# A decoder layer on one core: the scaling of the output weights, the copy of the inverse and two convolution taps take other places in their queues

## What is computed

```python
mixed = silu(causal_conv4(x @ w_qkv))        # 8192 channels: q, k (16 heads), v (32 heads)
z = x @ w_z                                  # 32 heads of 128
beta = sigmoid(x @ w_b)
g = -exp(A_log) * softplus(x @ w_a + dt_bias)
q, k = l2norm(q) * 128 ** -0.5, l2norm(k)    # each serves two heads of v
for t in range(128):                         # per sequence and head, S is 128 x 128
    S = S * exp(g[t])
    delta = (v[t] - k[t] @ S) * beta[t]
    S = S + outer(k[t], delta)
    o[t] = q[t] @ S
og = o * silu(z)
on = og * rsqrt(mean(og * og) + 1e-6) * norm_w
return on @ w_out                            # 4096 -> 256
```

## Time and profile before

| | before |
|---|---|
| median of 3 runs | 2258.57 us (2254.74 to 2260.40) |
| profiled execution, its own time | 2255.11 us |
| its span, first to last instruction | 2253.2 us |
| granted TensorE clock, mean | 0.970 |
| busy: PE, PEld | 93%, 76% |
| busy: DVE, ACT, POOL | 76%, 67%, 40% |
| ticks n=8 to 71 | 158 us to about 1722 us of the span |

### The profile page before, as it was taken

The page is one execution under the profiler, slowest core; times in us unless marked ns, Lnnn a source line. Parts: engine busy times, 40 slices in busy tenths (PEclk is TensorE's granted clock), DMA queues, the critical chain, the costliest instruction groups (busy, mean ns, idle before and its releaser), DMA issues.

```text
span 2253.2 us, 49295 instructions
## 1 busy us (share of the span) xinstructions
PE 2091.6 (93%) x18636; PEld 1716.1 (76%) x18636; DVE 1711.3 (76%) x2944; ACT 1512.7 (67%) x3585; POOL 904.1 (40%) x714
## 2 busy tenths in 40 slices
PE   4659999999999999999999999999988899999998
PEld 4448888888888888888888888887776476666776
DVE  6789797887879788787977978787325777767665
ACT  4547777777777777777777677775767666565632
POOL 1534454444445445445535534532333123213232
PEclk8779999999999999999999999998999999999999
DMA  3432322322232332233233222212243012322232
GB/s 77 94 73 48 89 44 72 63 64 67 55 85 46 72 75 49 68 60 80 52 70 72 48 70 56 75 34 56 58 137 133 1 66 76 104 94 73 91 136 85
DMA packets 274633, 161.56 MB, mean 72 GB/s; under 512 B 209352, under 2 KB 246752, under 8 KB 269280
## 3 DMA queue, kind: packets, MB, share of 16 engines
q1 hardware_dynamic: 274400, 158.41, 27.6%
HBM read 122.43 MB, written 35.91 MB: 70 GB/s over the span
## 4 chain that ended last, share of the span: by engine, by line
issue 36%; POOL 26%; PE 23%; DVE 8%; ACT 4%; DMA 2%; SPq 2%; POOLq 0%; DVEq 0%; ACTq 0%
POOL SM L577 5%; POOL EB L493 5%; POOL Q L555 5%; PE ps L1739 4%; POOL SZ L579 3%; PE ps L1347 3%; POOL EB L497 3%; PE ps L1349 3%; PE ps L1348 3%; POOL WL L471 2%; POOL SM L585 2%; PE ps L1660 1%; ACT SC L856 1%; PE ps L1651 1%; PE ps L1480 1%
## 5 line engine op out<-in xcount | busy, mean ns | idle before, releaser
L909 DVE SCALAR_TENSOR_TENSOR A<-ps,CW,A 128x508 f32<-128x508 f32 (+2 forms) x768 | 515.9, 734 | 55.3 <-ACT A L671 50.1
L572 POOL TENSOR_SCALAR SM<-SM 128x8 f32<-128x8 f32 x64 | 12.6, 196 | 813.8 <-ACT DL L690 813.8
L1480 PE MATMUL ps<-WO,DL 128*128 128x256 f32 x1008 | 244.5, 394 | 39.5 <-POOL WO L484 24.5
L1480 PEld LDWEIGHTS ps<-WO,DL 128*128 128x128 f32 x1008 | 189.7, 194 | 74.5 <-POOL WO L484 26.4
L1347 PE MATMUL ps<-XH,WH 128*128 128x512 f32 x512 | 221.5, 433 | 26.7 <-DVE A L909 25.8
L1127 DVE TENSOR_TENSOR SZ<-SZ,ps 128x512 f32<-128x512 f32 x128 | 87.7, 687 | 201.5 <-PE ps L1514 201.4
L1349 PE MATMUL ps<-XH,WL 128*128 128x512 f32 x512 | 206.4, 403 | 0.0
L1348 PE MATMUL ps<-XL,WH 128*128 128x512 f32 x512 | 205.2, 401 | 0.0
L690 ACT ACTIVATE DL<-SZ 128x128 f32<-128x128 f32 x512 | 152.4, 298 | 38.5 <-PE ps L1514 28.8
L856 ACT ACTIVATE SC<-ps,A 128x128 f32<-128x128 f32 x512 | 141.7, 386 | 51.5 <-DVE A L1252 50.7
L1112 DVE TENSOR_TENSOR BP<-ps,EB 128x512 f32<-128x512 f32 x256 | 158.3, 681 | 3.3 <-ACT EB L665 3.3
(11 more groups left out here) (225 smaller groups left out, 5556.1 us busy)
## 6 DMA issues: line engine op xcount, KB each, us to landing
EB<-decay_rows SPq DMA_DIRECT2D x128, 256.0 KB, 4.7
WE<-expert_halves SPq DMA_DIRECT2D x32, 1024.0 KB, 5.1
x_blocks<-BP SPq DMA_DIRECT2D x256, 32.0 KB, 1.7
X<-x_blocks SPq DMA_DIRECT2D x16, 512.0 KB, 6.5
tt_blocks<-TI SPq DMA_DIRECT2D x16, 512.0 KB, 2.6
tn_blocks<-TM SPq DMA_DIRECT2D x16, 512.0 KB, 2.6
TTF<-tt_blocks SPq DMA_DIRECT2D x256, 32.0 KB, 1.9
expert_halves<-BP SPq DMA_DIRECT2D x8, 1024.0 KB, 5.8
```

What stands on the lines that cost most here:

```text
L909: dve.scalar_tensor_tensor(acc, ps(i, 0, [[128, 4], [1, 128 - s]]), at(CW, tile * 4 + 3 - s, [[1, 1]]), acc, ALU.mult, ALU.add).then_inc(s ...
L1480: t = pe.matmul(ps(7 - i, b * 256, [[1, 256]]), at(on_buf(k), (4 * i + 2 * b + v) * 128, [[1, 128]]), at(WO, v * 256, [[1, 256]]), start=( ...
```

## The change

It moves the output weights WO by one tick. Their load is issued in ticks with k%4==3 (the last step that uses the old ones), at the end of SP's list for that tick, where it waits for that step's projections; before, it came first in the next tick. Their scaling on POOL is in the same tick, behind the decays and ahead of the norm section of step m. The power sk (L585) also goes ahead of the norm section. On ScalarE the copy of the inverse into TM goes from between the two on_T copies to behind the TTF copy. On DVE the taps kq_tap(n+1, 1) go from behind the gates to ahead of them, and kq_tap(n+1, 2) from the start of the next tick to the same place; the pumps' rooms are 5260 and 800 in place of 4060 and 2000 in the ticks below 64, and for n of 64 and more the same as before.

```diff
@@ -392,8 +392,6 @@
                 for n in range(NT):
                     m, k = n - LAG3, n - LAG4
                     vn = m + 1
-                    if 0 < k < NSTEP and k % 4 == 0:
-                        load_wo(k // 4)
                     if n % 4 == 0 and 4 <= n <= NSTEP:
                         load_x(n // 4 - 1)
                     if 0 <= m < NSTEP and m % 4 == 1 and m // 4 + 1 < HK:
@@ -411,6 +409,8 @@
                         store_x(n)
                     if n + 3 < NSTEP:
                         load_rows(n + 3)
+                    if 0 <= k and k % 4 == 3 and k + 1 < NSTEP:
+                        load_wo(k // 4 + 1)
                     if n == NSTEP + 1:
                         load_raw(0)
                         load_raw(1)
@@ -553,14 +553,21 @@
                         if n:
                             pool.wait_ge(sem["nq_mm"], n)
                         pool.tensor_tensor(at(Q2, 0, full), at(buf, 0, full), at(buf, 0, full), ALU.mult).then_inc(sem["sq"], 1)
-                    if 0 < k < NSTEP and k % 4 == 0:
-                        scale_wo(k // 4)
                     if EARLY - 1 <= n and n + 2 < NSTEP:
                         decay(n + 2)
                     if n == 5:
                         split_lo("v", W_V, 0)
                         split_lo("z", W_Z, 0)
                         scale_wo(0)
+                    if n % 4 == 0 and 4 <= n <= NSTEP:
+                        j = n // 4 - 1
+                        pool.wait_ge(sem["nk"], j + 1)
+                        if j >= 2:
+                            pool.wait_ge(sem["vv"], 4 * (4 * j - 4))
+                        pool.tensor_tensor(at(SM, C_SK + (j % 2) * 16, [[4, 4], [1, 4]]), at(SM, C_NK, [[4, 4], [1, 4]]),
+                                           at(SM, C_PH, [[0, 4], [1, 4]]), ALU.pow).then_inc(sem["sk"], 1)
+                    if 0 <= k and k % 4 == 3 and k + 1 < NSTEP:
+                        scale_wo(k // 4 + 1)
                     if m == NSTEP - 1:
                         pool.wait_ge(sem["ld_ctx"], 16)
                         pool.tensor_copy(at(EB, 0, [[9, 128], [1, 8]]), at(TI, 0, [[8, 128], [1, 8]])).then_inc(sem["cc"], 1)
@@ -577,13 +584,6 @@
                         pool.tensor_tensor(rr, xs, at(SM, C_MH, [[1, 8]]), ALU.pow).then_inc(sem["rr"], 1)
                         pool.wait_ge(sem["rr"], m + 1)
                         pool.tensor_tensor(szp, szp, at(SM, C_RR, [[1, 8], [0, 128]]), ALU.mult).then_inc(sem["on"], 1)
-                    if n % 4 == 0 and 4 <= n <= NSTEP:
-                        j = n // 4 - 1
-                        pool.wait_ge(sem["nk"], j + 1)
-                        if j >= 2:
-                            pool.wait_ge(sem["vv"], 4 * (4 * j - 4))
-                        pool.tensor_tensor(at(SM, C_SK + (j % 2) * 16, [[4, 4], [1, 4]]), at(SM, C_NK, [[4, 4], [1, 4]]),
-                                           at(SM, C_PH, [[0, 4], [1, 4]]), ALU.pow).then_inc(sem["sk"], 1)
                     if NSTEP - 4 <= k < NSTEP - 2:
                         x1_pow(k % 4)
                     if m == NSTEP - 2:
@@ -801,15 +801,15 @@
                         decay_exp(n + 1)
                     if s4 and k < NSTEP - 1:
                         on_T(k, 0)
+                    if s4 and k < NSTEP - 1:
+                        on_T(k, 1)
+                    if s3:
+                        act.wait_ge(sem["tt128"], m + 1)
+                        act.activation(at(TTF, 64, [[128, 8], [1, 64]], 0, 64), ps(6, 0, [[64, 8], [1, 64]], 0, 64),
+                                       ACT.Copy).then_inc(sem["tt128_sb"], 1)
                     if sv and vn % 4 == 0:
                         act.wait_ge(sem["inv"], INV_OPS * (vn // 4 + 1))
                         act.activation(at(TM, 0, [[1, 32], [32, 32]]), at(TI, 0, [[32, 32], [1, 32]]), ACT.Copy).then_inc(sem["tn"], 1)
-                    if s4 and k < NSTEP - 1:
-                        on_T(k, 1)
-                    if s3:
-                        act.wait_ge(sem["tt128"], m + 1)
-                        act.activation(at(TTF, 64, [[128, 8], [1, 64]], 0, 64), ps(6, 0, [[64, 8], [1, 64]], 0, 64),
-                                       ACT.Copy).then_inc(sem["tt128_sb"], 1)
                     if EARLY <= n and n % 2 and n + 1 < NSTEP:
                         decay_exp(n + 1)
                         decay_exp(n + 2)
@@ -1157,7 +1157,7 @@
                     vn = m + 1
                     s1, s3, s4, sv = n < NSTEP, 0 <= m < NSTEP, 0 <= k < NSTEP, 0 <= vn < NSTEP
                     rate = 1 if s1 else 2
-                    if s1 and (n > EARLY or n == 0):
+                    if s1 and n == 0:
                         kq_tap(n, 2)
                     if s1:
                         if n > EARLY or n == 0:
@@ -1168,8 +1168,10 @@
                         norm_rows(n - 1)
                     if n % 4 == 0 and 4 <= n <= NSTEP:
                         norm_sums(n // 4 - 1)
-                    pump(2500)
-                    pump(1560)
+                    if s1:
+                        pump(5260)
+                    else:
+                        pump(4060)
                     if sv:
                         v_tap(vn, 1)
                     if n % 4 == 0 and 4 <= n <= NSTEP:
@@ -1194,7 +1196,13 @@
                         y_add(k, 0)
                     if s4 and k < NSTEP - 2:
                         y_add(k, 1)
-                    pump(2000)
+                    if s1:
+                        pump(800)
+                    else:
+                        pump(2000)
+                    if EARLY <= n and n + 1 < NSTEP:
+                        kq_tap(n + 1, 1)
+                        kq_tap(n + 1, 2)
                     if s3:
                         gate(m, 0)
                     if s3:
@@ -1204,8 +1212,6 @@
                             apply_x1(0)
                     if NSTEP - 4 <= k < NSTEP - 2:
                         norm_x1(k % 4)
-                    if EARLY <= n and n + 1 < NSTEP:
-                        kq_tap(n + 1, 1)
                     if m == NSTEP - 2:
                         dve.wait_ge(sem["bias_tr"], 1)
                         dve.tensor_copy(q(0, [[1, 32]]), ps(3, 0, [[1, 32]])).then_inc(sem["bias_T"], 1)
```

More of the change, by code:

```diff
@@ L803, in _ @@
                         on_T(k, 0)
-                    if sv and vn % 4 == 0:
-                        act.wait_ge(sem["inv"], INV_OPS * (vn // 4 + 1))
-                        act.activation(at(TM, 0, [[1, 32], [32, 32]]), at(TI, 0, [[32, 32], [1, 32]]), ACT.Copy).then_inc(sem["tn"], 1)
                     if s4 and k < NSTEP - 1:
@@ L812, in _ @@
                                        ACT.Copy).then_inc(sem["tt128_sb"], 1)
+                    if sv and vn % 4 == 0:
+                        act.wait_ge(sem["inv"], INV_OPS * (vn // 4 + 1))
+                        act.activation(at(TM, 0, [[1, 32], [32, 32]]), at(TI, 0, [[32, 32], [1, 32]]), ACT.Copy).then_inc(sem["tn"], 1)
                     if EARLY <= n and n % 2 and n + 1 < NSTEP:
```

## The result

The kernel is slower. Beside 2256.65 us of the kernel before (4 runs, 2254.22 to 2260.40) it takes 2280.26 us (4 runs, 2277.09 to 2286.39): a ratio of 1.0106, interval 1.0086 to 1.0127. The profiled execution took 2279.98 us, with a span of 2278.2. The forecast of 2257.2 missed it by 23 us, and 2280 lies outside the range of 2243 to 2271.

The account below looks back on a forecast made before the run. PE's chain of waits, on WO scaling and the TTF copy, was taken to bound the kernel. Terms 4.6 + 0.3 - 1.0 - 5.4 - 0.9 + 1 = -1.4 us gave a 2257.2 us median, range 2243 to 2271.

Parts of the forecast that it names:

- the hold of DVE in the ticks n%4==1: DVE's L963 products fall inside POOL's shifted SZ product and wait: +0.4 us on the gates, bounds 0 and 1.3.
- the sum of -1.39 + 0.2 + 0.4 + 0.1: Ticks n%4==1: WO stall gone, SZ edge, DVE hold, taps ahead of the gates; together -0.7 us per tick.
- rival 3: Slower: the WO wait moves to POOL and PE waits at the SZ transposes; 2266 to 2273 us, chance 0.22.
- The ticks n%4==2: Two taps ahead of DVE's gates make u1, the first product with TA, later: +0.1 us per tick.
- The ticks n%4==0: Two taps ahead of DVE's gates make u1 later: +0.1 us per tick.
- The drain: Last ticks: -5.4 us at n=69 from the earlier WO load, -0.9 at n=67 from the moved TM copy.
- n=69: Drain tick where PE waits 7.4 us for WO; was to take the length of n=68: -5.4 us.
- n=67: Drain tick where moving the TM copy frees the longest TTF wait, with nothing behind it: -0.9 us.
- The start: The ramp, where DVE sets the pace, with 1200 less pump at the end of n=5: +1 us, bounds -1 and +4.
- the ticks n%4==3: TTF gain of 0.90 us lost through later ScalarE work, taps and gates, so u1 starts later: +0.84 us per tick.
- the stall on TTF: PE's wait for the TTF copy in ticks n%4==3, removed by moving the TM copy behind it: 0.90 us.

Follow-up runs that it names:

- g1: Kernel before with only POOL's scaling of WO moved ahead of Q2 (the square of q and k), behind the power: 2244.1 us, ratio 0.9956.
- e6: Kernel after with only DVE's pump rooms changed below tick 64, to 4060, 1700 and 800 from 5260, 500 and 800: 2256.8 us, ratio 1.0014 to before.
- e3: Kernel before plus DVE's part alone (pump rooms, and two taps of the next step ahead of the gates): 2299.5 us, ratio 1.0198.
- e1: Kernel before plus the WO part alone (load and scaling moved, the power ahead of the norm section): 2263.6 us, ratio 1.0044.
- e2: Kernel before plus the new order of ScalarE's two copies (TTF and inverse) alone: 2252.1 us, ratio 0.9992.
- e4: Kernel after with load and scaling of WO back at their old places, the power still ahead: 2291.8 us, ratio 1.0159 to before.
- i1: Kernel before plus the taps' part, with POOL's scaling of WO moved ahead of Q2 (the square): 2280.5 us, ratio 1.0104.
- e8: Kernel after with POOL's SZ product and q/k square cut to 64 elements in one tick of four, omitting needed work: 2254.4 us, ratio 1.0005 to before.

## Why the prediction was wrong

**The step that failed** is the hold of DVE in the ticks n%4==1: "+0.4 on the gates of this tick, with bounds of 0 (no hold) and 1.3 (a hold for the whole of SZ)". The mechanism was named, and the places were right: the pair was forecast inside the shifted SZ product and starts 0.24 us behind its beginning. The size was not. I had DVE wait for one operation of POOL. But the pair is two instructions, the power that used to lie behind SZ had been moved away by the same change, and so Q2 stood directly behind SZ and held the second product. The pair was 3.1 us longer in tick 41, and DVE's lateness reached PE by a way that the sum did not have: kq_proj waits 1.34 us for the v taps behind the pair, ahead of any gate. Step by step: the sum of -1.39 + 0.2 + 0.4 + 0.1 gave 24.6 us for the tick, 0.7 above PE's 23.86, and 26.1 came on average. So where the hold had 0.4 with an upper bound of 1.3, it took about 1.9 us of the tick. (In 3 of the 13, n = 29, 37 and 45, the load lands late and PE waits a microsecond at the SZ transposes instead, which is rival 3; one product is held, and they take 25.5 us from u1 to u1, the other ten 26.3.) The excess of 1.5 us times 13 is 20 us of the 23. Tick n=9, with both its pairs held, adds 3 us, and the ticks n%4==2 another 4; against them, the profile of the kernel before has one slow tick (n=57) of 1.7 us too much.

The Trainium skill (SBUF — State Buffer, Who interferes with whom), cited ahead of the run, states that such a DVE instruction and a GpSimd instruction reading SBUF exclude each other for the whole instruction, the first to come winning. The trace agrees, in both directions: DVE's second product waited for all of Q2, and Q2 took 2.34 instead of 1.89 us behind the first. It does not agree for the power of L585, which reads SBUF too: both products of the pair run inside it at 0.69 us each, in all 14 ticks of before and of g1 that have them there, so here the measurement decides. I quoted the rule and applied it to one instruction of two.

**The ticks n%4==2** had +0.1 and took +0.42. The cause is probably the same: the 256-element product of L974, 0.93 us when held by the end of an SZ product, is 2.16 long in tick 42 of after, behind a Q2 that starts 0.01 us ahead of it.

```profile
1018.31 1.90 POOL L555 TENSOR_TENSOR Q<-A 128x1024 f32<-128x1024 f32 x1
1018.32 2.16 DVE L974 TENSOR_TENSOR TM<-X,TI 128x256 f32<-128x256 f32 x1
```

It takes 2.16 us in all 12 ticks n%4==2 from n=14 to 58. In e6 it takes 1.51, and these ticks take 24.10 instead of 24.29. No run changed this hold alone.

**What held.** The stalls on WO and TTF are gone. WO lands 6.2 us behind its issue (6.1 forecast), and POOL waits for it. The ticks n%4==0 grew by 0.11 (0.1) and n%4==3 by 0.77 (0.84). The drain gave 6.1 us: n=69 takes 23.94 us (22.9 forecast), n=67 20.67 instead of 21.82. The start moved by 1.2 us (1 forecast), but one profile of each is little to go by: the seven profiles with the taps' part enter n=8 at 158.5 to 162.9 us (mean 161.0), the seven without at 155.9 to 160.7 (mean 158.2), so that the term is nearer 3, inside its bounds.

**Right for another reason in part: the ticks n%4==3.** The forecast gave all of their lateness to u1, through a ScalarE row 0.26 later and the two taps ahead of the gates. In tick 43 of after u1 waits 0.71 for the gates, and the transposes of v wait 0.69 for ScalarE's delta copies, which the forecast did not have (and the stall on TTF that it priced at 0.90 was a wait of 0.64 in tick 43). e3, with the inverse's copy at its old place, has 25.38 already: 0.63 of the 0.77 come with the two taps ahead of the gates, and 0.15 with the rest of the change. The place of the taps was right; that the whole came out within 0.1 us, with one wait missed and one priced too high, is partly luck.

**The rivals.** Rival 3 had the right sign and the right trigger (a POOL queue that stands for the load), with 0.22; its price went by PE's wait for SZ, and the larger one was DVE's. No case of mine had DVE's v taps late for kq_proj.

**How the parts add.** Alone they are +10 (e1), -2 (e2, inside its noise) and +45 us (e3). The sum of these is 53, but the three in one kernel cost 24, so that 29 us are in how they act on each other: beside the taps' part the WO part takes time off, since e4, which is after with the load and the scaling put back, is 11 us slower than after. e3 and after have nearly the same hold (3.4 and 3.2 us in tick 41); e3 has besides it the 1.8 us stall for WO with its slow clock, and a drain 7 us longer. i1 takes that stall out of e3 by another order and is 19 us faster than e3, though it frees one pair too. How the 29 divide between stall, clock and drain was not tried further.

## What to carry to other kernels

Where two engines exclude each other, a move is costed by what lies opposite it for its whole length, instruction by instruction: two short products can meet two long ones, and an operation that seems idle (a power on 16 elements) can be the gap that lets them through. Before a stall on loaded data is met by loading sooner, look at when the data landed: here it had long been there, and changing places with one queue neighbour gave what the earlier load could not. A pump's room, or any spacing by hand, is a parameter to be swept after each change of order, as it was worth 24 us here (only one other set of rooms was tried).

## What the runs showed of the hardware

- The power on 128 x 16 elements keeps POOL for 2.9 us and leaves DVE's two-input products at their full speed (the L963 pair 1.42 us under it, before and in g1). In e3 and i1, where it starts while a held product of DVE runs, it takes 3.35.
- DVE's taps, with one tensor in PSUM and one in SBUF, are not held: in after each takes 0.73 to 0.75 us with a long product of POOL beside it, and 0.70 to 0.79 without.
- POOL's operation with one SBUF input (L497, 1.35 us) holds DVE's product too: the second product of tick 33 in e8 starts 0.44 us behind it and takes 1.46 us instead of 0.69.
- The granted clock falls behind a stall of TensorE in some ticks and not in others with the same stall: behind 1.8 us for WO its mean over the tick is 0.94 in 6 of e3's 13 ticks n%4==1 (0.66 over 5 us of tick 49) and 1.00 in the other 7; before had it once (n=57, 26.95 instead of 25.25 us). What decides between them was not tried.
- A copy of 128 x 1024 elements in the inverse's reading order takes DVE 2.00 us, as long as ScalarE's 2.03.
